# A three-layer graph attention kernel: ten tiles of x loaded first, last sums read from PSUM, seven maxima of the next chunk at a chunk's end in place of five

## The reference

```
h = maximum(layernorm(x), 0);  x = x + gat(relu(gat(h, W1, ...)), W2, ...)
h = maximum(layernorm(x), 0);  x = x + gat(h, W3, ...)
gat: h = x @ W;  e = leaky_relu((h @ a_src)[src] + (h @ a_dst)[dst])
     ex = exp(e - segment_max(e, dst)[dst])
     out = segment_sum(ex * h[src], dst) / segment_sum(ex, dst) + b
```

## Time and profile before

| | |
|---|---|
| time, median of 3 runs (lowest to highest) | 682.75 us (681.59 to 683.83) |
| the profiled execution: time, span | 681.87 us, 680.1 us |
| granted TensorE clock, mean | 0.972 |
| VectorE busy | 637.0 us, 94% |
| TensorE busy (matmul) | 591.7 us, 87% |
| ScalarE, GpSimd busy | 483.2 us (71%), 459.4 us (68%) |
| longest waits of VectorE in the layers | 3.93, 3.46, 2.54, 2.40, 1.91 and 1.51 us |

### The profile page before, as it was taken

How to read it: one execution, slowest core, us unless ns; L and a number is a source line. 1 busy time by engine, 2 the same in 40 slices (tenths; PEclk the granted TensorE clock), 3 DMA queues, 4 the chain that set the end, 5 groups by cost and what they waited for, 6 DMA issues and landing times.

```text
span 680.1 us, 13823 instructions
## 1 busy us (share of the span) xinstructions
PE 591.7 (87%) x5571; PEld 574.7 (84%) x5571; DVE 637.0 (94%) x911; ACT 483.2 (71%) x719; POOL 459.4 (68%) x448
## 2 busy tenths in 40 slices
PE   1729855899979899999999999999989989999995
PEld 1628755799969799899989989898988989999994
DVE  3999999999999989999987999999998899999994
ACT  0416545556969778887666796979886699788891
POOL 5579101779928565775954685859698679596883
PEclk9978988799989999999999999999999999999998
DMA  2410002000000000000100100000010010010001
GB/s 73 118 55 2 1 8 15 25 2 1 20 1 1 20 1 20 1 2 8 28 12 1 27 1 21 1 19 1 8 21 19 1 27 12 29 33 7 20 1 42
DMA packets 22325, 12.07 MB, mean 18 GB/s; under 512 B 12393, under 2 KB 20055, under 8 KB 22255
## 3 DMA queue, kind: packets, MB, share of 16 engines
q1 hardware_dynamic: 21455, 9.85, 6.3%
q0 software_dynamic: 800, 1.26, 0.6%
HBM read 9.47 MB, written 1.64 MB: 16 GB/s over the span
## 4 chain that ended last, share of the span: by engine, by line
DVE 54%; PE 22%; issue 9%; DMA 5%; ACT 4%; POOL 4%; POOLq 0%; DVEq 0%
DVE scratch L952 21%; DVE ps L1068 17%; PE ps L1814 16%; DVE scratch L1150 6%; DMA xr<-in_x 3%; DVE ps L1070 2%; POOL scratch L752 2%; ACT scratch L1568 2%; ACT scratch L1570 2%; DVE ps L1080 1%; PE ps L1867 1%; PE ps L1845 1%; PE ps L1781 1%; DVE scratch L1068 1%; DMA gathered<-in_edges,start_i 1%
## 5 line engine op out<-in xcount | busy, mean ns | idle before, releaser
L1814 PE MATMUL ps<-hB,scratch 125*125 125x129 f32 x3450 | 403.9, 275 | 19.8 <-DVE scratch L1150 15.5
L1814 PEld LDWEIGHTS ps<-hB,scratch 125*125 125x125 f32 x3450 | 388.6, 187 | 28.6 <-DVE scratch L1150 21.2
L752 POOL TENSOR_TENSOR scratch<-scratch,C 125x625 f32<-125x625 f32 x239 | 303.9, 1283 | 110.9 <-ACT scratch L1570 108.9
L1068 DVE SCALAR_TENSOR_TENSOR ps<-C,a_unit,ps 125x625 f32<-125x625 fp8e3 x330 | 275.9, 867 | 2.3
L1568 ACT ACTIVATE scratch<-gathered,r_neg 125x625 f32<-125x625 f32 x219 | 176.4, 806 | 15.4 <-PE ps L1814 14.4
L1570 ACT ACTIVATE scratch<-scratch,r_src 125x625 f32<-125x625 f32 x219 | 178.9, 817 | 7.1
L1453 ACT ACTIVATE C<-ps 125x1000 fp8e3<-125x1000 f32 x80 | 78.3, 1000 | 77.2 <-PE ps L1781 77.2
L1781 PE MATMUL ps<-scratch 128*125 128x125 bf16 x1250 | 95.0, 241 | 32.0 <-DVE scratch L952 30.5
L1781 PEld LDWEIGHTS ps<-scratch 128*125 128x125 bf16 x1250 | 90.5, 156 | 35.8 <-DVE scratch L952 33.4
L1150 DVE SCALAR_TENSOR_TENSOR scratch<-ps,r_src,C 125x625 f32<-125x625 f32 x121 | 104.3, 862 | 5.1 <-PE ps L1804 5.1
L952 DVE TENSOR_TENSOR scratch<-key_lo,ps 128x4000 bf16<-128x4000 bf16 (+3 forms) x41 | 87.6, 2136 | 0.4 <-PE ps L1781 0.3
(11 more groups left out here) (195 smaller groups left out, 450.9 us busy)
## 6 DMA issues: line engine op xcount, KB each, us to landing
gathered<-g_lines SPq DMA_DIRECT2D x15, 305.2 KB
xr<-in_x SPq DMA_DIRECT2D x1, 1562.5 KB
out<-xr SPq DMA_DIRECT2D x4, 312.5 KB
edge_sb<-in_edges SPq DMA_DIRECT2D x1, 805.7 KB
gathered<-ext_lines SPq DMA_DIRECT2D x5, 122.1 KB
w<-in_W SPq DMA_DIRECT2D x2, 128.0 KB
out<-xr SPq DMA_DIRECT2D x1, 187.5 KB
out<-xr SPq DMA_DIRECT2D x1, 125.0 KB
```

The source lines that it names most:

```text
L752: g.tensor_tensor(slot[s], slot[s], C5[:, q % NC, s, :], ALU.mult).then_inc(pool_done, 1)
L1068: v.scalar_tensor_tensor(dest, counts, unit[:, s:s + 1], top, ALU.min, ALU.max).then_inc(S.top_done, 1)
L1814: last = mm(ps[0:P, acc_at(t):acc_at(t) + HW], A[:, P * t:P * (t + 1)], feat, start=opens and t in (0, 3), stop=closes, skip_group_check=True)
```

## The change

On SyncE, tiles 0 to 9 of x are asked for right behind the small transfer that starts the kernel, ahead of the weights; tiles 10 to 24 take the old place of x, followed by the two bias tables b2r and b3r, which leave the weights (13 transfers instead of 15) and now count with x. VectorE takes the statistics of the first ten tiles ahead of `first_keys`, and those of the other fifteen where all 25 stood. `AHEAD` becomes 7. In the last chunk the transposes of the maxima move from ahead of the last two tiles' matmuls to behind the matmuls of tile 21, ScalarE no longer copies the last sums, and VectorE reads them in PSUM.

```diff
-        N_WEIGHTS, N_CONSTS, KEY_STEPS = 15, 8, 9
+        N_WEIGHTS, N_CONSTS, KEY_STEPS = 13, 8, 9
-        AHEAD = 5
+        AHEAD = 7
+        X_FIRST = 10
@@ SyncE
             sp.dma_start(sample_i[:, :], apart[0, :, :]).then_inc(edges_in, 16)
+            sp.dma_start(xr[:, 0:X_FIRST, :], x_v[:, 0:X_FIRST, :]).then_inc(x_in, 16)
             sp.dma_start(w1[:, :], W1).then_inc(weights_in, 16)
...
-            sp.dma_start(b2r[:, :], b2.unsqueeze(0).broadcast_to([P, D])).then_inc(weights_in, 16)
-            sp.dma_start(b3r[:, :], b3.unsqueeze(0).broadcast_to([P, D])).then_inc(weights_in, 16)
             sp.wait_ge(first_in, 16)
-            sp.dma_start(xr[:, :, :], x_v).then_inc(x_in, 16)
+            sp.wait_ge(x_in, 16)
+            sp.dma_start(xr[:, X_FIRST:T, :], x_v[:, X_FIRST:T, :]).then_inc(x_in, 16)
+            sp.dma_start(b2r[:, :], b2.unsqueeze(0).broadcast_to([P, D])).then_inc(x_in, 16)
+            sp.dma_start(b3r[:, :], b3.unsqueeze(0).broadcast_to([P, D])).then_inc(x_in, 16)
@@ VectorE
             def node_statistics():
+                dve.wait_ge(x_in, 64)
+                for t in range(X_FIRST, T):
+                    last = v.bn_stats(bn6[:, t, :], xr[:, t, :])
...
+            def first_statistics():
                 dve.wait_ge(x_in, 16)
-                for t in range(T):
+                for t in range(X_FIRST):
                     last = v.bn_stats(bn6[:, t, :], xr[:, t, :])
                 last.then_inc(F.ln_lin, 1)
                 dve.wait_ge(F.ln_lin, 1)
+                for t in range(X_FIRST):
+                    v.bn_aggr(mv[:, t, :], bn6[:, t, :])
...
+            first_statistics()
             dve.wait_ge(first_in, 16)
             first_keys()
@@ last_result
                     if h == 0:
-                        dve.wait_ge(raw_half, Q)
+                        dve.wait_ge(acc_half, Q)
                     else:
-                        dve.wait_ge(F.raw_ready, Q)
-                    v.tensor_tensor(z0, raw[:, t0:t1, D], scale, ALU.mult).then_inc(F.z_lin, 1)
+                        dve.wait_ge(F.pe_done, Q * T)
+                    v.tensor_tensor(z0, acc3[h][:, :, D], scale, ALU.mult).then_inc(F.z_lin, 1)
...
-                        last = v.scalar_tensor_tensor(xt, raw[:, t, 0:D], rz[:, t:t + 1], xt, ALU.mult, ALU.add)
+                        last = v.scalar_tensor_tensor(xt, acc3[h][:, t - t0, 0:D], rz[:, t:t + 1], xt, ALU.mult, ALU.add)
@@ ScalarE
             factors(Q - 1)
-            move_sums(Q - 1, True)
@@ TensorE
                     elif s == T - 1:
-                        if q == Q - 1:
-                            top_transpose(F, q)
                         last_products(q)
+                    if q == Q - 1 and s == T - 4:
+                        top_transpose(F, q)
```

More of the change, by code:

```diff
@@ L510, in _ @@
                     sp.dma_start(v[:, i:i + 1], a.unsqueeze(1)).then_inc(weights_in, 16)
-            sp.dma_start(b2r[:, :], b2.unsqueeze(0).broadcast_to([P, D])).then_inc(weights_in, 16)
-            sp.dma_start(b3r[:, :], b3.unsqueeze(0).broadcast_to([P, D])).then_inc(weights_in, 16)
             sp.wait_ge(first_in, 16)
-            sp.dma_start(xr[:, :, :], x_v).then_inc(x_in, 16)
+            sp.wait_ge(x_in, 16)
+            sp.dma_start(xr[:, X_FIRST:T, :], x_v[:, X_FIRST:T, :]).then_inc(x_in, 16)
+            sp.dma_start(b2r[:, :], b2.unsqueeze(0).broadcast_to([P, D])).then_inc(x_in, 16)
+            sp.dma_start(b3r[:, :], b3.unsqueeze(0).broadcast_to([P, D])).then_inc(x_in, 16)
             sp.wait_ge(gather_in, 16 * (WG - 1))
-            sp.wait_ge(x_in, 16)
+            sp.wait_ge(x_in, 64)
             sp.dma_start(edge_sb[:, :, :], edges.rearrange("(p k) c -> p k c", p=P)).then_inc(edges_in, 16)
@@ L798, in last_bias @@
                 g.tensor_tensor(xc, xc, b3r[:, :].unsqueeze(1).broadcast_to([P, CT, D]), ALU.add).then_inc(b3_added, 1)
-            pool.wait_ge(weights_in, 16 * N_WEIGHTS)
+            pool.wait_ge(x_in, 64)
             backs(0, 0, T, 0)
@@ L899, in node_statistics @@
             def node_statistics():
+                dve.wait_ge(x_in, 64)
+                for t in range(X_FIRST, T):
+                    last = v.bn_stats(bn6[:, t, :], xr[:, t, :])
+                last.then_inc(F.ln_lin, 1)
+                dve.wait_ge(F.ln_lin, 2)
+                for t in range(X_FIRST, T):
+                    last = v.bn_aggr(mv[:, t, :], bn6[:, t, :])
+                last.then_inc(F.ln_stats, 1)
+            def first_statistics():
                 dve.wait_ge(x_in, 16)
-                for t in range(T):
+                for t in range(X_FIRST):
                     last = v.bn_stats(bn6[:, t, :], xr[:, t, :])
@@ L904, in node_statistics @@
                 dve.wait_ge(F.ln_lin, 1)
-                for t in range(T):
-                    last = v.bn_aggr(mv[:, t, :], bn6[:, t, :])
-                last.then_inc(F.ln_stats, 1)
+                for t in range(X_FIRST):
+                    v.bn_aggr(mv[:, t, :], bn6[:, t, :])
             def first_keys():
@@ L1137, in aggregate @@
             def aggregate(S, q):
-                dve.wait_ge(S.ln_lin, q % NC + 2)
+                dve.wait_ge(S.ln_lin, q % NC + (3 if S is F else 2))
                 for t in range(CT):
```

## The result

The changed kernel takes 684.24 us (median, 683.53 to 685.19) where the kernel before takes 682.33 beside it: ratio 1.0030, 95% interval 1.0021 to 1.0038. It is slower by some 1.9 us. That lies at the upper edge of the forecast of no change beyond 0.3% (682.9, up to 684.8); the interval holds 1.003, so by the ratio it is open whether the edge was passed. The profiled execution has a span of 681.8 us, 1.7 more than before.

What follows compares the result with a forecast made beforehand. VectorE bounds the count stage, VectorE and TensorE the layers, where block timing counts. Start -2.67, end -0.91 and -0.47, seven maxima +4.25 sum to +0.2 us, set against the median: 682.9 us, range 679.0 to 685.4.

Steps and rivals of the forecast that it cites:

- The start: Ahead of the first fetched edges: statistics of ten tiles move into VectorE's idle 6.40 us, -2.67 us.
- Rival 3: At the start: first x tiles land past 12.5 or fetched edges later than 15.2; 685.6 us, chance 0.07.
- The end: Last sums: no ScalarE copy, -0.91; moved transposes fill TensorE's waits, up to -0.47; together -1.4 us.
- Chunk 1 and chunk 3: Boundary into chunk 1 costs +0.26 us; new serial pair in chunk 3's maxima +0.15 (0 to 0.26).
- rival 5: At about eight boundaries: VectorE semaphores are free, so the net 0.26 falls away, -2.1; 680.8 us, chance 0.02.
- Chunk 4: VectorE's first blocks and the extremes come 1.81 us later and delay TensorE: +1.78 us, lower end +0.7.
- Chunk 5: Two extra maxima lie in VectorE's 2.54 row wait; VectorE is 0.78 earlier at tile 6: -0.50 us.
- Chunks 6 to 10: Boundary delays less returns, partly covered by VectorE's row waits and early blocks in chunk 10: together -0.03 us.
- Chunks 11 to 14: No VectorE waits before the last reduction: four boundaries less three returns, +2.59 us at the last chunk's tile 4.
- Rival 1: Across the chunks: delays don't add up, absorbed by waits, so faster, 680.5 or 678.7 us; chance 0.34.
- Rival 2: At the start: weights queue behind x and reach TensorE too late; 685.9 us at 3 us late, chance 0.08.
- rival 4: In each chunk: late TensorE frees slots later, holding back ScalarE and GpSimd; +2, 684.9 us, chance 0.06.

Runs made afterwards that it cites:

- the second experiment: The kernel before with only AHEAD raised from 5 to 7: 686.69 us, ratio 1.0067 to the kernel before.
- the third: The kernel before with only the new start, ten tiles of x and their statistics early: 680.40 us, ratio 0.9973 to the kernel before.
- experiment 6: The changed kernel with seven maxima ahead into chunks 5, 8, 9 and 10 and five into all others: 676.99 us, ratio 0.9927 to the kernel before.
- experiment 9: The changed kernel with seven ahead into chunks 0, 6, 7 and chunk 3's maxima placed as with seven, five into all others: 682.03 us, ratio 0.9993.
- experiments 5: The changed kernel with seven maxima ahead into chunk 4 only and five into all others: 681.44 us, ratio 0.9986 to the kernel before.
- the fourth: The kernel before with only the new end, last sums read from PSUM and transposes behind tile 21: 680.97 us, ratio 0.9979.
- The seventh: The changed kernel with seven maxima ahead into chunks 11 to 14 only and five into all others: 681.39 us, ratio 0.9991 to the kernel before.
- five: The changed kernel with AHEAD back at 5 everywhere, early x and last sums from PSUM kept: 678.38 us, ratio 0.9951 to the kernel before.

## Why the prediction was right, and where its terms were off

The forecast was little or no change, because a gain at both ends is eaten by later early blocks. That came true: the start and the end gain and the seven maxima cost, as foreseen. The time was 1.3 us too low; as a change, +0.2 was foreseen and +1.9 measured. The large misses are the start and chunks 6 to 10, each about 1 us.

The prediction named two signs of being wrong, and both came at least in part: the start gave less than 2.5, and in chunks 6 and 7 TensorE took up 0.8 of a late start of 1.8. Of its other signs, TensorE's early wait in chunk 14 is 0.47 and not 1 to 2 us, and the last reduction still waits 3.66, where 2 us of the 3.93 were to go; TensorE's weights, the first use of the last sums and the wait of 1.50 at chunk 5 are as foreseen. So the total is right in part by misses that offset each other, above all in chunks 6 and 7.

- **The start: -2.67 foreseen, -1.84 measured alone (1.2 to 2.5), and -1.5 by the traces.** The ten tiles landed at 10.0, in time; the weights too. What the working left out is the step "they move into the idle 6.40": it also moves what stands behind the statistics. `late_inside` came 3 us earlier and so beside GpSimd's product, 1.56 us lost, of which the absent wait for x gave 0.34 back: 2.67 - 1.56 + 0.34 = 1.45, and in the trace the first one-hots behind it start at 43.71 in place of 45.16, just that. The first maximum says the same: 197.95 in the second experiment with the old start, 196.46 in the third with the new one, neither behind a wait. By the Trainium skill (SBUF — State Buffer, the section "Who interferes with whom") a VectorE instruction with two SBUF inputs contends with a GpSimd instruction that reads SBUF; the trace agrees, with 2.75 against 1.19 us. The trace of before has such a stall too, at a negation of five values, beside a product of GpSimd that ended at 355.38; it takes 0.20 elsewhere:

```profile
354.68 0.73 DVE L1041 TENSOR_SCALAR r_neg<-r_src 125x5 f32<-125x5 f32 x1
```

  Rival 3 was half there as well: the first conversion of the fetched edges ended at 15.83 before and at 15.86 to 16.42 in the kernels that load x first, 0 to 0.6 later.
- **The end: -1.4 foreseen, -1.4 measured alone.** -0.90 for the copy and -0.54 for the transposes. In the changed kernel only the first is left, as experiment 2 shows. I had summed the -0.47 with a term that makes TensorE late, and lateness of TensorE is what takes GpSimd's wait away.
- **Chunk 1 and chunk 3: +0.26 and +0.15 foreseen; +0.25 and +0.14 measured.** Also the net 0.26 a chunk in steady state: chunk 13 costs 0.27. The prices from the earlier trace rows hold to a hundredth. This settles rival 5: by the Trainium skill (VectorE: DVE Perf Modes, the section on the DRAIN) a semaphore between VectorE's instructions is free; the runs disagree, and chunk 3, where only the place of one maximum and so its wait changes, costs 0.14 by that alone. Whether the semaphore costs it, or that each maximum reads the block just written, no run tells apart.
- **Chunk 4: +1.78 foreseen, +2.36 measured.** The 1.81 is there. Most of the rest is the negation, 0.44 longer beside GpSimd; with six ahead it isn't, and the chunk costs 0.98, near 0.91. Both chunk prices are good to 0.3.
- **Chunk 5: -0.50 foreseen, -0.76 measured.** It comes from the seven into 5 (experiment 6), not as a return of chunk 4's. VectorE is earlier there by more than the 0.78: the negation above takes 0.30 in the changed kernel in place of 0.73. What share of the 0.76 that has stays open.
- **Chunks 6 to 10: -0.03 foreseen, +0.92 measured.** This is the step that failed: "four boundaries at 1.81 less three returns of 1.55 is 2.59, less the row waits". Up to the end of chunk 7 the sum meets the measured time, 3.62 - 1.55 = 2.07 against 2.08, but by luck: it had neither the 0.8 that TensorE takes back at tile 14, nor the 0.81 of VectorE's stall beside GpSimd in chunk 6, and the two cancel (experiment 9). Behind chunk 7 I let the waits of 0.54 and 0.53 for rows swallow part of it. Those waits end on TensorE's rows, and TensorE was itself late, so they came later and stayed as long or grew (experiments 5 and 9). I had said that very thing of the wait at chunk 5, "no reserve: it hangs on TensorE", and not of these. What a wait for rows does cover is the two extra maxima that stand directly ahead of it: chunks 8, 9 and 10 gave 0.39, 0.24 and 0.54 back in the changed kernel, 1.17 in all.
- **Chunks 11 to 14: +2.59 foreseen, +2.31 measured.** Right in kind; chunk 11 bears 1.45 of it, the last only 0.07.
- **The clock.** The kernel before waited 0.54 for ScalarE's last counts ahead of the first maxima, the changed one not. That isn't the change: the second experiment, with the same code up to there, waited nothing at a mean granted clock of 1.00 in 190 to 200, and the fourth 1.06 at 0.66. In the sixth experiment's trace TensorE's last counts ran at a mean granted clock of 0.66 in 190 to 200, so in good part at 1.2 GHz (window: us, busy of PE, PEld, DVE, ACT, POOL, then clock), and VectorE waited 1.05:

```profile
190.00:200.00 10.00, 8.02 (x82) 7.58 (x81) 8.88 (x10) 6.05 (x7) 0.00 (x0) 0.66 0.01 2
```

```profile
193.09 5.66 PE L1796 MATMUL ps<-scratch 128*125 128x125 bf16 x58 [1.67 <-DVE scratch L968]
...
197.86 0.87 DVE L1086 TENSOR_SCALAR ps<-C,a_unit 125x625 f32<-125x625 fp8e3 x1 [1.05 <-ACT C L1469]
```

  The seventh, with the same code up to there, waited 0.52 (clock 0.83), and the fifth nothing (clock 0.91). A profile's own execution so carries 0 to 1.06 us of luck at this place.

Summed from the traces: -1.75 to the first maximum without that wait (196.35 against 198.64 - 0.54), -0.54 for the wait, -0.90 at the end, and +0.28 + 0.14 + 2.18 - 0.76 + 0.92 + 2.30 = +5.06 for the seven (from the table, changed kernel against five). The kernel before differs from five in two chunks: its chunk 4 took 35.00 in place of 35.29, +0.29, and its last chunk, with the transposes not moved, 29.91 in place of 29.36, -0.55. Together +1.6, where the spans differ by 1.7 and the medians by 1.9.

Rival 1, the delays not adding up, held in part: chunks 5, 8, 9 and 10 are shorter with seven everywhere, and within chunks 6 and 7 TensorE takes back 0.8. Rival 2 had no part, since TensorE's weights were in time. Of rival 4 two small waits of TensorE for GpSimd's blocks show in the ninth experiment, 0.27 and 0.34, right behind the places where it had taken time back.

## What to carry to other kernels

A wait is a reserve only against lateness of the engine that waits, and only directly ahead of it; where it ends on an engine that is late by the same cause, it moves along and covers nothing. The waits of the late engine itself, later in the same chunk, are a reserve for it. Before work is put "ahead", ask at each boundary which of the two it meets, and set the amount by boundary. And when instructions move in time, look at what else runs beside them in their new place: a small VectorE instruction with its operands in SBUF, begun inside a long one of GpSimd, can last until that one's end: in these runs 0.96 us in place of 0.16, and 1.21 in place of 0.17. A sum that fits can hide such a stall, as that of chunks 6 and 7 did.

## What the runs showed of the hardware

- In every trace of this case the negations of float32 in SBUF (5 or 15 elements a partition) and the small products of two SBUF operands that were stretched beside a GpSimd product ended 0.02 to 0.03 us after its end: 0.61 in place of 0.16, 0.96 in place of 0.16, and 1.21 in place of 0.17 at 500.32 in the changed kernel. None of them began inside such a product and ended inside it. The product with 1024 elements took 2.00 to 3.08 us in place of 1.19, ending 1.08 to 1.09 behind GpSimd's in all nine traces where it began inside it. Statistics (0.28 each), comparisons of one value a partition (0.25) and instructions with one operand from PSUM (one-hots 2.20, blocks 0.87) ran beside GpSimd at their usual length. GpSimd's own product was not longer for it (2.37 beside VectorE's, 2.38 before).
- SyncE's next issue behind the ten tiles of x took 4.57 us, where the same transfer's issue took 0.37 before, and the one behind the fifteen tiles 11.52. Both long issues come right behind a large transfer of the same engine; that this is the cause is not shown. Nothing here needed the queue; the small transfers' issues ended at 11.9 in place of 8.1.
- Reading the last sums from PSUM in place of SBUF: the three take 0.87 us, and took 0.88, and the small product ahead of them 0.17 both times, so there is no sign of the 0.26 that the prediction worked out from the cited section.
